# A fused two-layer kernel: one of two plain block products of the first layer replaced by a seven-product form

## What is computed

```python
base  = einsum('bsi,oi->bso', x, W0) + bias            # W0: 2048 x 2048
low   = einsum('bsi,bri->bsr', x, A[itok7])            # rank 16, adapter picked per batch
x     = x + base + scale[itok7][:, None, None] * einsum('bsr,bor->bso', low, B[itok7])
out   = x + einsum('bij,bkj->bik', x, W1[itok14])      # one of 16 2048 x 2048 weights per batch
```

## Time and profile before

| | before |
|---|---|
| median of 3 runs | 2594.73 us |
| the profiled execution | 2594.02 us |
| its span | 2592.2 us |
| TensorE busy in the span | 2558.9 us, 12250 matmuls |
| VectorE busy | 2119.0 us |
| ScalarE busy | 1386.6 us |
| GpSimd busy | 761.4 us |
| DMA, mean rate | 265 GB/s |

### The profile page before, as it was taken

How to read it: one execution, slowest core, us unless ns; L and a number is a source line. 1 busy time by engine, 2 the same in 40 slices (tenths; PEclk the granted TensorE clock), 3 DMA queues, 4 the chain that set the end, 5 groups by cost and what they waited for, 6 DMA issues and landing times.

```text
span 2592.2 us, 35474 instructions
## 1 busy us (share of the span) xinstructions
PE 2558.9 (99%) x12250; PEld 2117.4 (82%) x12250; DVE 2119.0 (82%) x1926; ACT 1386.6 (53%) x1478; POOL 761.4 (29%) x614
## 2 busy tenths in 40 slices
PE   8999999999999999979999999999999999999999
PEld 7888888888888888768888888888888888888887
DVE  6568999997988999878788787787878887787865
ACT  3234433334344333456676676666766666666755
POOL 5554332342333324111220230231311312213311
PEclk9999999999999999989999999999999999999999
DMA  9996642863676538768778678677899999999896
GB/s 359 348 380 203 203 132 100 274 211 130 182 248 205 158 116 274 276 224 272 257 260 281 240 254 300 234 272 274 276 355 363 349 358 357 350 323 327 307 326 227
DMA packets 213714, 686.19 MB, mean 265 GB/s; under 512 B 23424, under 2 KB 31776, under 8 KB 213536
## 3 DMA queue, kind: packets, MB, share of 16 engines
q1 hardware_dynamic: 204032, 649.33, 69.9%
q0 software_dynamic: 9216, 33.56, 6.7%
q10 hardware_dynamic: 288, 1.05, 0.1%
HBM read 650.29 MB, written 100.66 MB: 290 GB/s over the span
## 4 chain that ended last, share of the span: by engine, by line
PE 93%; DMA 3%; DVE 2%; SPq 1%; issue 0%; ACT 0%; POOL 0%; ACTq 0%; DVEq 0%; POOLq 0%
PE acc L1290 18%; PE acc L1291 18%; PE acc L1292 18%; PE acc L1207 13%; PE acc L1209 13%; PE acc L1208 13%; PE acc L1246 1%; PE acc L1224 1%; DVE ws L1161 1%; DMA xst<-xt 1%; DVE tx L1161 1%; DMA bias_s<-bias 1%; DMA y<-acc 1%; DMA ystage<-xt 0%; DMA wb<-w 0%
## 5 line engine op out<-in xcount | busy, mean ns | idle before, releaser
L1161 DVE TENSOR_TENSOR ws<-wb,ws 128x1024 fp32r<-128x1024 f32 x968 | 1254.0, 1322 | 291.3 <-ACT ws L997 275.0
L997 ACT CAST ws<-wb 128x1024 fp32r<-128x1024 f32 x968 | 991.1, 1050 | 793.8 <-PE acc L1292 484.5
L1290 PE MATMUL acc<-ws,ops 128*128 128x512 f32 (+1 forms) x2048 | 800.5, 391 | 14.6 <-DVE ops L1161 12.3
L1291 PE MATMUL acc<-ws,ops 128*128 128x512 f32 (+1 forms) x2048 | 798.2, 390 | 0.0
L1292 PE MATMUL acc<-ws,ops 128*128 128x512 f32 (+1 forms) x2048 | 797.7, 389 | 0.0
L907 POOL TENSOR_TENSOR wb<-wb,eye_s 128x128 f32<-128x128 f32 x384 | 333.7, 900 | 1162.2 <-DMA wb<-w 1162.0
L1207 PE MATMUL acc<-tx,ws 128*128 128x512 f32 x1600 | 623.3, 390 | 4.4 <-DVE tx L1161 2.8
L1209 PE MATMUL acc<-tx,ws 128*128 128x512 f32 x1600 | 622.5, 389 | 0.0
L1208 PE MATMUL acc<-tx,ws 128*128 128x512 f32 x1600 | 622.5, 389 | 0.0
L1290 PEld LDWEIGHTS acc<-ws,ops 128*128 128x128 f32 x2048 | 385.0, 188 | 93.9 <-issue 18.0
L1292 PEld LDWEIGHTS acc<-ws,ops 128*128 128x128 f32 x2048 | 384.9, 188 | 81.3
(11 more groups left out here) (67 smaller groups left out, 1018.6 us busy)
## 6 DMA issues: line engine op xcount, KB each, us to landing
wb<-w SPq DMA_DIRECT2D x816, 512.0 KB, 6.3
xb<-x SPq DMA_DIRECT2D x78, 512.0 KB, 5.5
xb<-x POOLq DMA_DIRECT2D x64, 512.0 KB, 8.8
y<-acc SPq DMA_DIRECT2D x32, 1024.0 KB, 10.7
wb<-w_sums SPq DMA_DIRECT2D x64, 512.0 KB, 7.7
out<-ost SPq DMA_DIRECT2D x128, 256.0 KB, 7.4
xst<-xt SPq DMA_DIRECT2D x60, 512.0 KB, 5.9
ystage<-y SPq DMA_DIRECT2D x60, 512.0 KB, 7.3
```

The costliest lines, as they stand in the source:

```text
L997: eng.copy(hi, src).then_inc(s_hi, 1)
L1161: eng.tensor_tensor(lo, src, hi, ALU.subtract).then_inc(s_lo, 1)
L1290: eng.matmul(dst, yh, wh, start=begin, stop=False)
L1291: eng.matmul(dst, yh, wl, start=False, stop=False)
```

## The change

Big product 1 takes the form `Seven` in place of `Eight`; `PLAIN` holds only 0. `MADE_FROM` goes from 10 to 9 and `MADE_EVERY` from 18 to 15, so the planned times of the eight sets of weight sums run from 9 to 114 us in place of 10 to 136 us. As the first layer then has 99 steps, the two sets of PSUM banks are met in the other order from the start, and three places that named a bank are written so that they follow (`acca`, `put_bank`, the warm-up matmuls).

```diff
-MADE_FROM = 10.0
-MADE_EVERY = 18.0
+MADE_FROM = 9.0
+MADE_EVERY = 15.0
...
-PLAIN = (0, 1)
+PLAIN = (0,)
 FORM = [Eight if q in PLAIN else Seven for q in range(NG * K)]
...
-        acca = bank[7]
+        acca, put_bank = (bank[7], bank[6]) if SETS[0] == 0 else (bank[3], bank[2])
...
-                    eng.tensor_copy(sorted_f[:], bank[6][:, 0:NB]).then_inc(s_order, 1)
+                    eng.tensor_copy(sorted_f[:], put_bank[:, 0:NB]).then_inc(s_order, 1)
...
-                eng.matmul(bank[0][:], tx[:, 0, 0, 0:P], tx[:, 0, 0, 0:512], start=True, stop=True)
+                eng.matmul(bank_at(0, 0)[:], tx[:, X_SLOT[0], 0, 0:P], tx[:, X_SLOT[0], 0, 0:512], start=True, stop=True)
...
-                        eng.matmul(bank[6][:, 0:NB], wide, put, start=True, stop=True).then_inc(s_put, 1)
+                        eng.matmul(put_bank[:, 0:NB], wide, put, start=True, stop=True).then_inc(s_put, 1)
```

## The result

The changed kernel takes **2610.09 us** (median of 4 runs, 2608.93 to 2613.46); the kernel before, run beside it, 2594.59 us. The ratio is 1.006, interval 1.0048 to 1.0073: 15.5 us slower. The forecast was 2600.9 us and its range ended at 2608. The profiled execution is one of 2608.93 us, 14.9 us above that of before.

A forecast was written before the change was run, and what follows sets the result against it. The prediction took TensorE, busy 99% of the span, as the bound, with VectorE late in big product 1. 2594.0 - 10.9 + 17.1 = 2600.2 us, forecast as 2600.9 since the profiled run lay 0.7 under the median; range 2585 to 2608.

The forecast's parts named there:

- The price of 2.2 us for a hold: Each VectorE split beside a GpSimd sum is held up by 2.2 us, taken for 14.5 operations before step 12.
- the 1.2 of the earlier trace: Low end: 1.2 us per GpSimd operation, from splits at 120 to 149 us where VectorE is idle half the time.
- the count in the budget: Before step 12, VectorE has 38.2 us of own work and 14.5 holds, 31.9 us, from 93.15 us: through at 163.2.
- the clock at 0: Lower TensorE clock behind up to four waits: 5 us at most, taken as 0 and kept for the range.
- waits at the change of layer: The 12.3 us wait there is for splits of `ops` behind the low-rank part and goes on as it is.
- step removed: TensorE in big product 1: 48 matmuls less, 10.9 us off, all on the path.
- delay at step 12: TensorE starts step 12 17.1 us late, VectorE being through at 163.2 us against 146.1.
- Rival 1: Outer sums fall beside evictions and into idle time, 1.2 us each: delay 3.2 us, time 2587.0 us; chance 0.27.
- Rival 3: Second s3 stands behind two accumulating DMAs waiting for loads of x: delay 22 to 25 us, 2606 to 2609; chance 0.15.
- Its sign: The mark that would show the larger delay: a TensorE wait that goes back to line 881.
- Rival 2: DMAs, full from 75 to 190 us, are the bound: no gain and no loss, 2594.7 us; chance 0.13.
- its high end: Delay at step 12 with 2.4 us for each operation and 5 us of slower clock: 25 us.

The follow-up runs named there:

- small_moves: Changed kernel with the loads of weight-sum sets 2 to 7 cut to 64 of 1024 columns, sums whole: 2611.42 us, ratio 1.007.
- vec_late8: Changed kernel with the outer weight sums of sets 4 to 7 moved from GpSimd to VectorE, planned 8 us later: 2599.25 us, ratio 1.0022.
- tiny_sums: Changed kernel with GpSimd's outer weight sums (m1 to m4) done on 8 of 1024 columns, all loads, stores and waits kept: 2585.96 us, ratio 0.9969.
- before_tiny: Kernel before the change with its 32 outer weight sums on GpSimd done on 8 of 1024 columns: 2590.66 us, ratio 0.9987.
- vec_spread: `vec_mix` with the sums of sets 6 and 7 planned at 131 to 144 us: 2592.81 us, ratio 0.9994.
- vec_mix: Changed kernel with outer sums of sets 4 to 7 on VectorE, planned 4 us later, and two inner sums of big product 1 there too: 2592.94 us, ratio 0.9997.
- old_spacing: Changed kernel with `Seven` kept in big product 1 but the sets' spacing back at 10 and 18: 2618.69 us, ratio 1.0095.

## Why the prediction was wrong in size and right in kind

**Right.** TensorE's waits are for splits of VectorE at line 1207; VectorE is busy without a gap from 94 us; splits take 3.4 us beside GpSimd's sums, at 2.2 us each; evictions are not held; 48 matmuls are 10.9 us; after step 12 only 2.0 us are lost in the first layer, 1.5 of them clock, and nothing is given back. The chance was on slower, and it is slower. The marks it had named: waits of 17 us from 105 to 160 us (14.3 there and 4.4 at 167), the last line 899 at 165 us (167.48), the first product with `w_sums` at 196 us (about 206: step 12 plus three steps and 1.5). The price of 2.2 us for a hold, against the 1.2 of the earlier trace rows, was the right choice: VectorE had no idle time. (TensorE's waits in the kernel before add up to 29.5 us and not to 27; nothing rests on it.)

**Wrong: the count in the budget.** The step that failed is "15 operations; the first [...] meets VectorE only half. 14.5 x 2.2 = 31.9 us". The trace has 18 operations that held VectorE before step 12 could start: m3 of set 4 (at 93.33 us, thought to be over), the second s3, and m4 of set 7 came on top, and the first met VectorE in full. That is 3.5 x 2.2 = 7.7 us more. The two that met in one split, s3 and m4, cost 5.4 where two turns cost 4.4: 1.0 more. 31.9 + 7.7 + 1.0 = 40.6 us of holds; 93.0 + 38.2 + 40.6 = 171.8 us, which is when step 12 started (171.81), against 163.2 forecast. I had cut GpSimd's list at the operations that step 12 *needs* (m1 and m2 before s3). What counts is what GpSimd *reaches* before VectorE is through, and since each hold puts off that time, the list must be taken on until the two agree. By the order's own rows the second s3 and m4 of set 7 stand close behind m3, so one more round of the sum should have found these two of the three.

**Wrong: the clock at 0.** Before step 12 the forecast's reason held, the 7.0 us are inside VectorE's delay. Behind step 12's wait 1.5 us are on the path. Shorter waits at the change of layer (2.7 us) more than pay for that, and I had costed them at nothing.

| term, us | forecast | measured |
|---|---|---|
| step removed | -10.9 | -10.9 |
| delay at step 12 | +17.1 | +25.7 |
| clock behind it | 0 | +1.5 |
| first layer after, not followed | 0 | +0.5 |
| second layer | 0 | -1.9 |
| sum against 2594.0 | 2600.2 | 2608.9 |

**The rivals.** Rival 1 (gaps): refuted; a GpSimd sum cost 40.6 / 18 = 2.3 us, above the 1.8 at which the change breaks even. Rival 3 named the size (delay of 22 to 25 us), but not the reason: the second s3 did stand behind two accumulating DMAs, and these issued in 1.92 us without a wait for a load. Its sign was half there: ScalarE's copy for the second weight half of step 12 waited 6.55 us for line 881, but TensorE's wait at 171.81 us ended with the split of the first half, which VectorE's work and the holds made late. Rival 2 (DMAs, no gain and no loss) is refuted for this kernel by `small_moves`; but something like it lies beneath. The complete kernels that took most of the port's delay away ended at 2592.8 to 2596.0 us (`vec_late8`, with its sums later still, at 2599.3), and rival 2 had said 2594.7. That the times agree is in part luck: port holds and late buffers have a share in what is left. The range was too narrow above because its high end took more per operation and more clock, but never more operations.

**What stays open.** Why GpSimd had two turns in a row at 165 us and VectorE eleven at 103 us, when otherwise they mostly alternate. And whether loads moved ahead of 60 us, or buffers of x freed sooner, would bring the gain of some 5 us that `tiny_sums` shows against `before_tiny`; no run tried either. No complete version ran measurably faster than the kernel before; the best, `vec_spread` and `vec_mix`, are equal to it.

## What to carry to other kernels

A step saved on TensorE is worth only what the engines and DMAs that feed it can also do without: here 10.9 us on paper, some 5 without the outer sums' holds, -15 with them. When VectorE has no idle time, each sum that GpSimd "takes over" costs VectorE twice what doing it itself would (2.2 against 1.14 us), so such sums belong beside evictions, into idle time, or on VectorE. And when one engine's delay is computed from another's list of work, go on down that list until its time and the delay agree.

## What the runs showed of the hardware

Who is next at the shared port was not expected. Beside a GpSimd sum of 2.4 us a VectorE operation with two SBUF inputs is held for 2.2 us, and an eviction for nothing; where both engines have work back to back they mostly alternate, 3.34 us for a pair. But one GpSimd sum waited while eleven VectorE operations went by and took 15.78 us, and one VectorE split was held by two GpSimd sums and took 6.65 (another, in `old_spacing`, 6.18). The Trainium skill, "SBUF — State Buffer", section "SBUF: two separate sides", calls the port pair an exclusive lock for the whole instruction, taken by whichever starts first. The hold of 2.2 us for a sum of 2.4 us agrees with it but for 0.2 us. The same section says that issue order decides who blocks. That does not cover these rows: the GpSimd sum stood ready at 102.67 us, before eleven of the operations that went by it. So neither alternation nor issue order can be counted on.

TensorE's clock: behind four of the five waits (2.9 to 5.2 us) it fell to the lower level, 0.50 granted in 112 to 114, 155 to 157 and 172 to 174 us; behind the one of 2.6 us it stayed at 1.00. Over the four it cost 7.8 us more, 1.5 to 3.0 each. It lay beneath the VectorE bound except for the last 1.5, but where TensorE is the bound a wait of 3 to 5 us can cost some 2 us on top. It need not: in `small_moves` the clock stayed at 1.00 behind a wait of 3.48 us and in `vec_mix` behind one of 2.98, while in `vec_late8` it was 0.52 and 0.63 in the 4 us behind one of 2.29 us. The wait's length alone does not tell.
